# Sorted row tiles for three batches and a dense fourth batch in place of a dense expert network

## The reference, cut to what matters

```python
x = x + xattn(layernorm(x), ctx)          # softmax over clipped scores
flat = layernorm(x).reshape(1024, 128)
scores = softmax(flat @ router_weight.T + router_bias)
topk_w, topk_idx = top_k(scores, 2)
gu = einsum('th,ehn->ten', flat, gate_up_proj) + gate_up_bias
gate, up = minimum(gu[..., :256], 7), clip(gu[..., 256:], -7, 7)
act = (up + 1) * gate * sigmoid(1.702 * gate)
down = einsum('tei,eih->teh', act, down_proj) + down_bias
x = x + (take_along_axis(down, topk_idx) * topk_w).sum(axis=1)
```

## Time and profile before

| | us |
|---|---|
| median of 3 runs | 156.82 (156.45 to 157.28) |
| the profiled execution | 156.96 |
| its span | 155.2 |
| busy in it: TensorE / VectorE / ScalarE / GpSimd | 149.2 / 103.2 / 100.8 / 49.8 |

### The profile page before, as it was taken

How to read it: one execution, slowest core, us unless ns; L and a number is a source line. 1 busy time by engine, 2 the same in 40 slices (tenths; PEclk the granted TensorE clock), 3 DMA queues, 4 the chain that set the end, 5 groups by cost and what they waited for, 6 DMA issues and landing times.

```text
span 155.2 us, 3023 instructions
## 1 busy us (share of the span) xinstructions
PE 149.2 (96%) x1004; PEld 136.0 (88%) x1004; DVE 103.2 (66%) x288; ACT 100.8 (65%) x205; POOL 49.8 (32%) x49
## 2 busy tenths in 40 slices
PE   7998799999999999999999999999999999999993
PEld 7988699999999999989988888788888888887892
DVE  0668958386859595963683899957654377552773
ACT  3183878657484736468866656957788677779450
POOL 1356529243505300210067643312333321233020
PEclk9999999999999999999999999999999999999999
DMA  4979999700000000000000000000000000000022
GB/s 116 371 292 404 388 401 384 225 1 4 0 2 0 4 0 0 4 0 2 0 0 4 0 0 0 0 4 0 2 0 0 0 0 0 0 4 0 4 68 68
DMA packets 5909, 10.69 MB, mean 69 GB/s; under 512 B 380, under 2 KB 3080, under 8 KB 5896
## 3 DMA queue, kind: packets, MB, share of 16 engines
q1 hardware_dynamic: 4968, 10.00, 17.9%
q10 hardware_dynamic: 928, 0.53, 1.2%
HBM read 10.00 MB, written 0.52 MB: 68 GB/s over the span
## 4 chain that ended last, share of the span: by engine, by line
PE 78%; DVE 10%; POOL 4%; ACT 3%; issue 3%; DVEq 0%
PE T L1147 14%; PE O L1041 13%; PE S L944 11%; PE S L946 10%; PE S L945 10%; PE T L1025 6%; PE S L951 3%; POOL ex L309 2%; DVE xT L847 2%; DVE up L838 1%; PE S L1147 1%; DVE w_lo L779 1%; DVE sc L631 1%; ACT pr L419 1%; POOL rstd L287 1%
## 5 line engine op out<-in xcount | busy, mean ns | idle before, releaser
L838 DVE TENSOR_SCALAR up<-up 128x512 f32<-128x512 f32 x32 | 13.9, 434 | 24.7 <-ACT up L504 24.7
L350 POOL TENSOR_TENSOR x<-x,xn 128x512 f32<-128x512 f32 x13 | 17.3, 1331 | 38.6 <-ACT xn L524 38.6
L427 ACT ACTIVATE pT<-T 128x512 f32<-128x512 f32 (+1 forms) x32 | 15.4, 513 | 18.4 <-PE T L1025 18.4
L524 ACT ACTIVATE xn<-T,w_scaled 128x128 f32<-128x128 f32 x56 | 16.1, 374 | 17.2 <-PE T L1147 14.1
L944 PE MATMUL S<-x_hi,w_hi 128*128 128x512 f32 x64 | 26.8, 419 | 0.2 <-DVE w_lo L779 0.2
L1041 PE MATMUL O<-pT,ctx_sb 128*128 128x128 f32 (+1 forms) x208 | 25.9, 275 | 0.2 <-ACT pT L427 0.2
L945 PE MATMUL S<-x_lo,w_hi 128*128 128x512 f32 x64 | 25.3, 395 | 0.0
L946 PE MATMUL S<-x_hi,w_lo 128*128 128x512 f32 x64 | 25.3, 395 | 0.0
L1041 PEld LDWEIGHTS O<-pT,ctx_sb 128*128 128x128 f32 (+1 forms) x208 | 24.6, 192 | 0.6 <-ACT pT L427 0.5
L631 DVE TENSOR_SCALAR_CACHE_REDUCE sc<-S,clip_hi 128x400 f32<-128x400 f32 (+1 forms) x32 | 18.9, 630 | 8.7 <-PE S L946 8.5
L498 ACT ACTIVATE keysT_sb<-S,gate_bias 128x512 f32<-128x512 f32 x32 | 22.7, 708 | 1.7 <-PE S L946 1.6
(11 more groups left out here) (127 smaller groups left out, 248.4 us busy)
## 6 DMA issues: line engine op xcount, KB each, us to landing
keysT_sb<-in_ctxT SPq DMA_DIRECT2D x3, 801.0 KB, 9.9
ctx_sb<-in_ctx SPq DMA_DIRECT2D x3, 768.0 KB
gu_sb<-in_gu SPq DMA_DIRECT2D x1, 2048.0 KB, 14.9
ctx_sb<-in_ctx SPq DMA_DIRECT2D x3, 256.0 KB, 4.5
x_sb<-in_x ACTq DMA_DIRECT2D x1, 384.0 KB, 5.0
keysT_sb<-in_ctxT SPq DMA_DIRECT2D x1, 289.0 KB, 5.5
out_x<-xn SPq DMA_DIRECT2D x1, 256.0 KB, 2.3
out_x<-xn SPq DMA_DIRECT2D x2, 128.0 KB, 1.8
```

Of the source, the lines that this page charges most:

```text
L350: nc.gpsimd.tensor_tensor(acc, acc, y_sb[:, k % 2, :], ALU.add).then_inc(y_added, 1)
L524: ins = nc.scalar.activation(y_sb[:, k % 2, t * DIM:(t + 1) * DIM], T[k % 2][:, t * DIM:(t + 1) * DIM], ACT.Copy, scale=w_scaled[:, bass.d ...
L838: nc.vector.tensor_scalar(up[:, k % 2, ih, :], up[:, k % 2, ih, :], 2.0 * LIMIT, 1.0 - LIMIT, ALU.min, ALU.add).then_inc(up_clipped, 1)
```

## The change

Batches 0 to 2 (768 tokens, each sent to 2 experts, 1,536 rows) are sorted by expert. Each expert's rows are padded to whole tiles of 128 rows; with 8 experts that is at most 19 tiles (`SLOTS`). While attention runs, VectorE ranks the experts of each token (`rank_experts`), TensorE counts with matmuls on triangular and all-ones matrices how many rows of each expert precede a token (`count_before`), VectorE makes the row numbers (`find_rows`), and GpSimd writes each normalised token, with the number of its result row behind it, to two rows of a DRAM tensor by indirect DMAs (`send_rows`, four DMAs of 128 rows to a batch). That tensor is first filled with ones (`blank_rows`, SP). `tile_table` finds for each of the 19 tiles its expert and its first row. SP reads a first row into a register, and loads the tile; TensorE reads the expert's column into a register and slices the weights by it.

A tile is: transpose of the rows, split by ScalarE and VectorE, one gate/up product of 512 columns (a bias matmul and three matmuls), silu on ScalarE, clip and product on VectorE, two transposes, a copy, `down`, a copy, and an indirect DMA of GpSimd to the token's result row in a second DRAM tensor (`send_result`). At the end SP loads the results and VectorE adds them with the two routing weights (`sum_results`).

Batch 3 stays dense, as 8 expert steps of 256 tokens behind the tiles. The split weights of all 8 experts stay in SBUF: loaded over the keys as these come free (`expert_weights` on SP), split by ScalarE (`weights_hi`) and GpSimd (`weights_lo`) during attention. Two `gate_up` halves no longer stand in the last tile of attention, and between `project_v(last)` and the first tile TensorE has no instruction (`GAP = 0`). The all-ones tile of 1,419 columns takes the place of the zeroed tile of 128 columns in the warm-up.

The diff, cut to its core:

```diff
+SPARSE = [0, 1, 2]
+DENSE = 3
+RT = len(SPARSE) * TPB
+RTOK = RT * P
+SLOTS = RT * TOP_K + EXPERTS - 1
+ROWS = (EXPERTS - 1) * RTOK + (SLOTS - RTOK // P) * P
+ROW = DIM + 1
+DEST = DIM
...
+GAP = 0
+X2_LAST = 2
+WEIGHED = SPARSE + [DENSE]
...
-            sp.dma_start(gu_sb[:].rearrange("p (e n) -> p e n", e=EXPERTS), gu.rearrange("e h n -> h e n")).then_inc(gu_in, 16)
+            sp.dma_start(bias_raw[:], ffn_bias).then_inc(bias_in, 16)
...
+            def blank_rows():
+                sp.wait_ge(blank_ready, 1)
+                n = ROWS // (P * PAD_ROWS)
+                sp.dma_start(xs.rearrange("(p c r) d -> p c (r d)", p=P, c=n),
+                             ones[:].unsqueeze(1).to_broadcast([P, n, PAD_ROWS * ROW])).then_inc(pads_in, 16)
+            def expert_weights(k):
+                e0, n = W_PARTS[k]
+                sp.wait_ge(keys_lo_ready, (k + 1) * NCH)
+                sp.dma_start(keysT_sb[:, k, 0:n * 2 * HIDDEN].rearrange("p (e n) -> p e n", e=n),
+                             gu[e0:e0 + n].rearrange("e h n -> h e n")).then_inc(w_in[k], 16)
+            blank_rows()
+            expert_weights(0)
+            expert_weights(1)
+            expert_weights(2)
+            sp.wait_ge(first_row_ready, 1)
+            for i in range(SLOTS):
+                at = sp.value_load(first_row[0:1, i:i + 1], min_val=0, max_val=ROWS - P)
+                if i == 0:
+                    for s in range(len(SPARSE)):
+                        sp.wait_ge(rows_sent[s], 16 * TOP_K * TPB)
+                sp.dma_start(xt[:, i, :], xs[bass.ds(at, P), :]).then_inc(xt_in[i], 16)
...
+            nc.gpsimd.memset(later[:], 1.0).then_inc(route_consts, 1)
+            nc.gpsimd.memset(upto[:], 1.0).then_inc(route_consts, 1)
+            nc.gpsimd.memset(low_row[:], -1.0).then_inc(route_consts, 1)
...
+            def weights_lo(e):
+                k = next(k for k, (e0, n) in enumerate(W_PARTS) if e0 <= e < e0 + n)
+                at = (e - W_PARTS[k][0]) * 2 * HIDDEN
+                s = slice(e * P, (e + 1) * P)
+                pool.wait_ge(w_hi_ready, e + 1)
+                nc.gpsimd.tensor_tensor(w_lo[:, :, s], keysT_sb[:, k, at:at + 2 * HIDDEN].rearrange("p (c n) -> p c n", c=WIDTH),
+                                        w_hi[:, :, s].bitcast(F32), ALU.subtract).then_inc(w_lo_ready, 1)
+            def copy_payload(b):
+                pool.wait_ge(xn2_ready, b + 1)
+                nc.gpsimd.tensor_copy(xp[:, b, 1, :, 0:DIM], xp[:, b, 0, :, 0:DIM]).then_inc(payload_copied, 1)
...
+                for c in choices:
+                    for t in range(TPB):
+                        k = c * TPB + t
+                        nc.gpsimd.indirect_dma_start(xs[:, :], bass.IndirectOffsetOnAxis(ap=row_of[:, s, k:k + 1], axis=0),
+                                                     xp[:, SPARSE[s], c, t, :], None, bounds_check=ROWS - 1,
+                                                     oob_is_err=False).then_inc(rows_sent[s], 16)
+            def send_result(i):
+                pool.wait_ge(y_ready, i + 1)
+                nc.gpsimd.indirect_dma_start(yb[:, :], bass.IndirectOffsetOnAxis(ap=xt[:, i, DEST:DEST + 1].bitcast(I32), axis=0),
+                                             y_sb[:, i % Y_RING, :], None, bounds_check=TOP_K * RTOK - 1,
+                                             oob_is_err=False).then_inc(y_sent[i % Y_RING], 16)
...
             keys_lo(2, 1)
+            first_send()
             root2(0)
+            copy_payload(0)
             keys_lo(3, 0)
+            weights_lo(0)
+            weights_lo(1)
+            weights_lo(2)
             keys_lo(3, 1)
+            weights_lo(3)
             root2(1)
+            copy_payload(1)
+            send_rows(0)
+            pool.wait_ge(chosen_ready, 2)
+            weights_lo(4)
+            weights_lo(5)
+            weights_lo(6)
+            weights_lo(7)
             root2(2)
+            send_rows(1)
+            copy_payload(2)
+            send_rows(2)
             root2(3)
...
+            router_exponentials(2)
+            for i in range(SLOTS):
+                send_result(i)
+                if i == 4:
+                    router_exponentials(3)
...
             keys_hi(3, 0)
+            weights_hi(0)
+            weights_hi(1)
             copies(3)
             exponentials(4)
             copy_oT(1)
             keys_hi(3, 1)
+            weights_hi(2)
+            weights_hi(3)
             copies(4)
             exponentials(5)
             split_x2(1)
+            weights_hi(4)
+            weights_hi(5)
             copies(5)
             exponentials(6)
             copy_oT(2)
+            weights_hi(6)
+            weights_hi(7)
             copies(6)
             exponentials(7)
...
+            for k in range(-2, SLOTS + 2):
+                if 0 <= k - 2:
+                    evict(k - 2)
+                if 0 <= k - 1 < SLOTS:
+                    copy_act(k - 1)
+                if k + 2 < SLOTS:
+                    split_rows(k + 2)
+                if 0 <= k + 1 < SLOTS:
+                    silu(k + 1)
+                if k == X2_LAST:
+                    split_x2(last)
+            for e in range(EXPERTS):
+                dense(e)
+                if e in (0, 1):
+                    copy_wT(e)
...
+            def tile_table():
+                dve.wait_ge(counted, 1)
+                link(nc.vector.tensor_reduce(tiles_of[:], full[:], AX.X, ALU.add))
+                nc.vector.tensor_scalar(gap[:], tiles_of[:, 0:EXPERTS - 1], -float(P), float(RTOK), ALU.mult, ALU.add)
+                link(nc.vector.tensor_tensor(tiles_upto[:], upto[:], tiles_of[:].unsqueeze(1).to_broadcast([P, EXPERTS - 1, EXPERTS]),
+                                             ALU.mult))
+                link(nc.vector.tensor_reduce(last_of[:], tiles_upto[:], AX.X, ALU.add))
+                shape = [P, SLOTS, EXPERTS - 1]
+                link(nc.vector.tensor_tensor(passed[:], tile_no[:].unsqueeze(2).to_broadcast(shape),
+                                             last_of[:].unsqueeze(1).to_broadcast(shape), ALU.is_ge))
+                link(nc.vector.tensor_reduce(expert_no[:], passed[:], AX.X, ALU.add))
+                link(nc.vector.tensor_tensor(passed[:], passed[:], gap[:].unsqueeze(1).to_broadcast(shape), ALU.mult))
+                link(nc.vector.tensor_reduce(skipped[:], passed[:], AX.X, ALU.add))
+                nc.vector.scalar_tensor_tensor(first_row[:], tile_no[:], float(P), skipped[:], ALU.mult,
+                                               ALU.add).then_inc(first_row_ready, 1)
+                nc.vector.tensor_scalar(expert_at[:], expert_no[:], float(P), None, ALU.mult)
+                nc.vector.tensor_scalar(bias_pick[:], expert_no[0:BIAS_ROWS, :], bias_expert[:, 0:1],
+                                        None, ALU.is_equal).then_inc(table_ready, 1)
...
+            nc.vector.memset(ones[:], 1.0).then_inc(blank_ready, 1)
...
+            split_bias()
+            scale_down_bias()
...
+            split_x2(last - 1)
+            add_router_bias(last - 1)
+            rank_experts(last - 1)
+            invert_sums(last)
+            add_regions(last - 1)
+            find_rows(last - 1)
+            compare_counts()
+            logit_maximum(last - 1)
+            logit_differences(last - 1)
+            tile_table()
+            residual(last)
+            residual_moments(last)
+            for k in range(-2, SLOTS - 1):
+                if k + 2 < SLOTS:
+                    split_rows(k + 2)
+                if 0 <= k + 1:
+                    clip_up(k + 1)
+                    product(k + 1)
+                if k == 0:
+                    payload(last)
+                if k == X2_LAST:
+                    split_x2(last)
...
+                if k == 6:
+                    rank_ties(last)
+                if k == 8:
+                    rank_count(last)
+                if k == 9:
+                    expert_weights(0)
+                if k == 11:
+                    expert_weights(1)
+                if k == 13:
+                    expert_weights(2)
+                if k == 15:
+                    expert_weights(3)
...
+            def count_before(s):
+                dst = COUNTS[s][:, PFX:PFX + TPB * EXPERTS].rearrange("p (t e) -> p t e", e=EXPERTS)
+                pe.wait_ge(route_consts, ROUTE_CONSTS)
+                if COUNTS[s] is O:
+                    pe.wait_ge(oT_copied, s + 2)
+                else:
+                    pe.wait_ge(logit_ready, s + 1)
+                pe.wait_ge(chosen_ready, s + 1)
+                nc.tensor.matmul(dst, later_r[:], chosen[:, s, 1:1 + TPB, :], start=True, stop=False)
+                ins = nc.tensor.matmul(dst, ones_r[:], chosen[:, s, 0:TPB, :], start=False, stop=(s == 0))
+                if s:
+                    pe.wait_ge(summed_before, s)
+                    before_it = sent_before[:, s, :].unsqueeze(1)
```

(60 more changed lines are left out.)

## The result

The changed kernel took 171.44 us, median of 4 runs (166.29 to 177.04), beside 157.05 us for the kernel before in the same series: slower, by a ratio of 1.0595 (95% interval 1.0539 to 1.0652). The prediction was 152.1 us, in a range of 146.5 to 161.

A forecast was written before the change was run, and what follows sets the result against it. TensorE, full at full clock, was taken to bound both stages, its work falling 19.7 us. Delays and idle brought the first tiles to 89.7, the remaining tiles 37.5, dense batch to 148.3, span 150.5: 152.1 us, range 146.5 to 161.

The forecast's parts named there:

- Work of a tile, 1.71 us: Sorted tiles on TensorE: transposes, four 512-column matmuls with the bias among them, and fp32 down take 1.71 us a tile.
- Clock, 1.9 us charged once: First tiles behind the idle stretch: the first two gate/ups run at half pace, charged once at 1.9 us.
- Rival 3: Tile loop: clock stays at 1.2 GHz through the tiles after the idle stretch, giving 183 us; chance 0.04.
- The router's wait in the tiles, 1.5 us: Tile loop: router(3) waits 1.5 us for splits that ScalarE and VectorE issue behind tile 3's work.
- Idle ahead of the first tile, 6.5 us: Between project_v(3) and the first tile, TensorE idles 6.5 us for counts, four sends at 1.1 us and two DMA landings.
- Rival 1: GpSimd's indirect sends bind if slow: 2.2 us each gives 163 us, deciding from 1.95 us a send; chance 0.16.
- Start, +1.2 us: Kernel start: TensorE's first work waits for a VectorE memset grown from 128 to 1,419 elements, 1.2 us later.
- Attention, +1.2 us: Attention: weights_lo ahead in GpSimd's queue delays root2(1), so batch 1's normalisation and transpose come 1.2 us later.
- The turn, -0.2 us: From batch 2's transpose to project_v(3): gate/up matmuls leave, but waits, counts and uncovered copies leave only 0.2 us gained.
- Bursts of VectorE, 3.8 us: Tile loop: four expert_weights and two ranking halves exceed VectorE's slack and cost 3.8 us, bounds 0 and 5.
- rival 2: Tile loop: the tile's chain through ScalarE and VectorE binds at a 2.2 us period, giving 157.1 us; chance 0.15.
- Dense batch and end: Behind the tiles: batch 3's dense steps with the add take 21.1 us, then 2.2 us to the span's end.

The follow-up runs named there:

- experiment 6: Bias operands of the tiles zero-padded from 16 to 128 partitions, on top of the fillers of experiment 5; 157.97 us, ratio 1.0063 to the kernel before.
- experiment 10: On top of experiment 9, ones set in two pieces and batch 3's router one tile later without filler; 153.16 us, ratio 0.9771 to the kernel before.
- experiment 7: On top of experiment 6, GpSimd's weights_lo(2) and weights_lo(3) moved behind batch 1's second key half, root and payload copy; 156.97 us, ratio 0.9962.
- experiment 11: Kernel of experiment 10 with the tiles' bias operands on 16 partitions again; 157.47 us, ratio 1.0062 to the kernel before.
- experiment 3: Changed kernel with the filler of experiment 2 and constant expert numbers on TensorE, no register reads in the tile loop; 172.46 us.
- experiment 4: Changed kernel with all 19 expert register reads ahead of the tiles, then 14 filler matmuls; 179.51 us, ratio 1.1312 to the kernel before.
- experiment 9: On top of experiment 7, 2 fillers ahead of batch 2's transposition and 4 ahead of its router; 155.13 us, ratio 0.9899 to the kernel before.
- experiment 12: Kernel of experiment 10 without any filler; 154.85 us, ratio 0.986 to the kernel before.
- experiment 5: Changed kernel with 32 fillers behind the last projection, 5 and 4 at the first tiles, 6 ahead of batch 3's router; 162.07 us, ratio 1.0337.
- experiment 8: Changed kernel with only the bias operands padded to 128 partitions, no filler; 158.98 us, ratio 1.0138 to the kernel before.
- experiment 2: Changed kernel with 28 filler matmuls in the idle stretch behind the last projection; 167.38 us, ratio 1.0498 to the kernel before.
- experiment 1: Changed kernel once more, no edit; 174.44 us median (164.61 to 178.53).

## Why the prediction was wrong, step by step

The two terms that failed by most are the work of a tile and the clock. The prediction had named a tile period over 2.1 us as a sign of being wrong, and it came. With both put right in the tiles and nothing else changed (experiment 6) the kernel takes 157.97 us, level with the kernel before and 5.9 above the predicted 152.1; in that profile `project_v(3)` ends at 81.4 us, predicted at 78.2, so the start, attention and the turn were together short by 3.2 us as well, half clock in the turn included. That the kernel of experiment 10, at 153.16 us, stands only 1.1 above the prediction is partly luck: experiments 7 and 10 also took away costs that the prediction had counted, at the start, in attention and at the router.

- **Work of a tile, 1.71 us: the step that failed, by 4.3 us.** I priced the bias matmul at 0.23 us "among" four of 512 columns. On 16 partitions the transposition ahead of it held the pace for 0.20 us, the bias for 0.42 and the next matmul for 0.34; with 128 partitions they hold it for 0.03, 0.32 and 0.23. That is 0.38 us a tile; experiments 6, 10 and 11 show it, and with 128 partitions the loop runs at 1.70 to 1.71. The bound of 0 to 0.5 us a tile that I gave to the register reads had the size and the wrong cause (experiment 3). The kernel before has nothing like it in its steady expert steps: its few small-partition matmuls stand outside the rows I read. The Trainium skill, "TensorE: Matmul & The Clock Gate", section "LDWEIGHTS (loading the stationary operand)", says that a load on few partitions takes as long as one on 128; the traces agree, 0.18 and 0.19 us. The Trainium skill, "TensorE: Matmul & The Clock Gate", section "The mechanism", says that a load is pulled ahead of matmuls in flight where it goes to another row group or to the spare weight buffer, and lists the overlap only for row groups that differ; the rows of experiments 3 and 10 show loads running ahead between matmuls on the same 128 partitions and held back between 16 and 128, so by that list the padding would have brought nothing, and the measurement decides.
- **Clock, 1.9 us charged once: the step that failed, by 4 to 15 us.** Rival 3, with a chance of 0.04, was the nearest to what happened: half clock in the tiles, not all of them. My reason against it, that "the tile loop fills TensorE like attention", was wrong twice: TensorE's busy column reads 10.00 of 10.00 at half clock and says nothing, and the loop had 0.4 us in each tile in which no weight load ran, and a wait at the router. The clock fell at three places: ahead of the tiles (the profile after), at `router(3)` (experiment 4) and in the turn (experiment 9). With the padding the falls cost 1.7 us (experiment 12), about what I had charged; it was the loop on 16 partitions, slow to get the clock back, that made them dear. The Trainium skill, "TensorE: Matmul & The Clock Gate", section "HAM oscillation", whose warning of half clock behind an idle wait I had cited and priced too low, was borne out: 0.50 from 85 to about 126 us.
- **The router's wait in the tiles, 1.5 us.** TensorE waited 1.06 us there in experiment 4: right in kind, a little high. (The 4.08 us of that tile in experiment 5 hold fillers and the router's own matmuls besides.) I had not seen that it also costs the clock.
- **Idle ahead of the first tile, 6.5 us: right.** 6.75 us measured, from 81.76 to 88.51. The sends hold GpSimd 0.97 to 0.98 us each, at a pace of 1.27 us, for my 1.1, so 4.8 us for the four where I had 4.4; scatter and load took 3.6 us where I had 4.0. Rival 1, which needed 1.95, did not come, but the stretch that it fears exists: one send of batch 0, beside VectorE's clip of 1,601 columns at 58.9 us, held GpSimd for 1.46.
- **Start, +1.2 us: right as far as can be told.** The first matmul came 1.34 us later. The first transposition of normalised tokens, behind the loads, came 0.7 us later in the profile after, and 0.3 to 1.6 in the ten profiles with this start; the kernels of experiments 10 to 12 have it 0.8 us or more ahead of these.
- **Loads, 0: right.** ScalarE's `weights_hi` were not held up by the store of ones.
- **Attention, +1.2 us: right at its place, short as a whole.** Batch 1's transposition came 2.25 us later, of which 0.7 is the start, so 1.5 us. My order of GpSimd's queue was right; that VectorE's clip would double beside it was not foreseen (I expected VectorE to be quiet), nor the second wait of 0.92 us. Experiment 7 won 1.0 us at batch 1.
- **The turn, -0.2 us: wrong.** From batch 2's transposition to `project_v(3)` the kernel of experiment 5, at full clock, took 8.5 us from start to start, the kernel before 8.14; the matmuls taken away had covered the waits, and on half clock it was 10.1 us in the profiled execution.
- **Bursts of VectorE, 3.8 us: near in sum once the loop is fast, in part for another reason.** In the slower loop the rankings and the weights cost 0.2 to 0.4 us each; at 1.71 us the longer periods of experiment 10 (2.53, 3.03 and six of 1.89 to 2.06) sum to 3.6 us over the steady one. Of these, 1.3 us are not shown to be VectorE's: in the period of 3.03 TensorE waited 1.05 us for ScalarE's copy, and ScalarE had been idle 2.4 us for TensorE's results.
- **Tile chain (rival 2), 2.2 us a tile: not the cause.** Its number agrees with what was measured, but the chain let 1.70 us pass as soon as TensorE could.
- **Dense batch and end.** 21.1 and 2.2 us predicted; from the last `down` of a tile (126.7 us) to the last VectorE operation (149.07) experiment 10 took 22.4 us, and 2.3 us to the end of the span.

The steps measured in order: fillers 166.3 to 162.1, padding to 158.0, GpSimd's order and the turn to 155.1, ones and router to 153.2. The first of these starts from the lower level of the changed kernel, and experiments 6 and 8 show that the first two overlap: the padding alone gives 159.0, so that the fillers on top of it win 1.0.

## What to carry to other kernels

Price each matmul of a new loop by a row of its own shape, partitions included: a matmul on 16 partitions among matmuls on 128 cost 0.38 us a tile, its neighbours' share included, and zeros in the other 112 partitions cost nothing that showed. Where a change takes away the work that filled TensorE at a junction, look for every stretch in which it then mostly waits, not only the longest: three of them dropped the clock here, and the loop with the matmul on 16 partitions kept the half clock for 20 to 48 us. A busy column near 100% does not show that; the granted clock and the records per microsecond do.

## What the runs showed of the hardware

- A weight load ran ahead of the matmul in flight between 128-partition matmuls (0.11 us apart) and not between a 16-partition one and its neighbours (0.17 and 0.24 us without a load).
- The clock fell to half behind 2.5 us of waits within 3.1 us (experiment 2), behind a wait of 1.06 us and six matmuls of 8 columns (experiment 4), and behind two waits of 0.65 and 0.75 us with six such matmuls (experiment 7). It came back under the 14 fillers of experiment 4, in the second or third tile of the padded loop (experiments 8 and 12), and only after 6 to 12 tiles of the loop with 16 partitions (the changed kernel, experiments 1 to 4).
- A register read on TensorE takes 0.69 us where nothing covers it, and nothing that could be measured in the loop.
- An indirect send of 128 rows holds GpSimd 0.98 us, one every 1.27 us, and held it 1.46 us beside VectorE's clip of 1,601 columns. That clip took 1.96 us beside GpSimd's split of 512 columns, and 1.05 us without it.
